# Attention over 39 fields: probabilities transposed as 32 fp32 products of 39x39 blocks in 64x64 tiles, in place of eight 103x103 transposes

## What is computed

```python
def _mhsa(x, Wq, Wk, Wv, Wr):          # x: [2048, 39, 64], HEADS = 2, dh = 32
    q = (x @ Wq).reshape(B, n, HEADS, dh)
    k = (x @ Wk).reshape(B, n, HEADS, dh)
    v = (x @ Wv).reshape(B, n, HEADS, dh)
    scores = jnp.einsum('bihd,bjhd->bhij', q, k)
    attn = jax.nn.softmax(scores, axis=-1)
    out = jnp.einsum('bhij,bjhd->bihd', attn, v).reshape(B, n, D)
    return jax.nn.relu(out + x @ Wr)
embed_x = emb_table[X + offsets[None, :]]
att = embed_x
for i in range(3):
    att = _mhsa(att, WQ[i], WK[i], WV[i], WR[i])
att_output = relu(att.reshape(B, FLAT) @ Wlin)
h = relu(embed_x.reshape(B, FLAT) @ W1 + b1)
h = relu(h @ W2 + b2)
dnn_output = relu(h @ W3 + b3)
return sigmoid(att_output + dnn_output)
```

## Time and profile before

| | |
|---|---|
| median of 3 runs | 2034.81 us |
| runs | 2032.1, 2036.02, 2034.81 us |
| span of the profiled execution | 2034.7 us |
| PE, multiplications busy | 94% |
| PE, weight loads busy | 83% |
| DVE busy | 83% |
| ACT busy | 66% |
| POOL busy | 44% |
| mean granted TensorE clock | 0.991 |

### The profile page before, as it was taken

How to read it: one execution, slowest core, us unless ns; L and a number is a source line. 1 busy time by engine, 2 the same in 40 slices (tenths; PEclk the granted TensorE clock), 3 DMA queues, 4 the chain that set the end, 5 groups by cost and what they waited for, 6 DMA issues and landing times.

```text
span 2034.7 us, 105018 instructions
## 1 busy us (share of the span) xinstructions
PE 1914.9 (94%) x44960; PEld 1692.9 (83%) x44960; DVE 1690.5 (83%) x3771; ACT 1351.5 (66%) x3609; POOL 893.3 (44%) x949
## 2 busy tenths in 40 slices
PE   1499999999999999999999999999999999999998
PEld 0387888888888888888888888888888888888887
DVE  3477889889898888979888898888889898888987
ACT  1366666667666676766766776666776667676665
POOL 6544354444535454354544435354453545444000
PEclk9899999999999999999999999999999999999998
DMA  4210111111111111111111111111111111110000
GB/s 113 60 31 25 31 27 32 29 30 31 28 33 28 31 30 29 32 28 32 29 30 30 29 33 27 32 28 30 31 28 34 28 32 29 30 31 26 20 20 16
DMA packets 67859, 64.71 MB, mean 32 GB/s; under 512 B 24056, under 2 KB 54792, under 8 KB 67400
## 3 DMA queue, kind: packets, MB, share of 16 engines
q1 hardware_dynamic: 47432, 37.52, 6.3%
q0 software_dynamic: 19968, 20.49, 5.3%
HBM read 27.24 MB, written 0.01 MB: 13 GB/s over the span
## 4 chain that ended last, share of the span: by engine, by line
PE 86%; DVE 5%; issue 4%; ACT 3%; another core or an unknown queue 1%; POOL 1%; SPq 0%; DMA 0%; ACTq 0%
PE SV L479 20%; PE Ob L496 14%; PE X L464 12%; PE X L457 8%; PE X L459 5%; PE X L458 5%; PE Mb L432 3%; PE Mb L433 3%; PE Mb L434 3%; PE Ob L457 3%; PE Ob L458 2%; PE Ob L459 2%; PE Ob L423 2%; PE Mb L450 1%
## 5 line engine op out<-in xcount | busy, mean ns | idle before, releaser
L355 POOL DMA_INDIRECT emb<-L_rec_emb_table,idx_t x624 | 646.9, 1037 | 752.4 <-PE Ob L496 551.2
L742 DVE TENSOR_REDUCE den<-sd 103x16 f32<-103x624 f32 x384 | 308.0, 802 | 225.6 <-ACT sd L616 211.0
L479 PE MATMUL SV<-yv,xs 64*39 64x142 f32 x12288 | 456.0, 285 | 21.2 <-ACT v_sb L618 13.4
L479 PEld LDWEIGHTS SV<-yv,xs 64*39 64x39 f32 x12288 | 349.8, 113 | 68.0 <-issue 39.6
L600 ACT ACTIVATE xs<-Ob 128x312 f32<-128x312 f32 x256 | 110.4, 431 | 383.6 <-PE Ob L496 383.6
L722 DVE TENSOR_REDUCE mx<-SV 103x8 f32<-103x312 f32 x768 | 332.7, 473 | 37.0 <-PE SV L479 28.7
L496 PEld LDWEIGHTS Ob<-pt,v_sb 39*32 39x32 f32 x12288 | 272.1, 106 | 96.5 <-issue 96.0
L464 PE MATMUL X<-ident,pn 103*103 103x103 f32 x3072 | 343.0, 255 | 0.0
L496 PE MATMUL Ob<-pt,v_sb 39*32 39x39 f32 x12288 | 326.4, 198 | 8.9 <-issue 8.5
L332 POOL COPY xs<-embT 64x256 f32<-64x256 f32 x300 | 239.1, 797 | 211.6 <-ACT embT L560 80.7
L727 DVE TENSOR_TENSOR sd<-SV,mx 103x312 f32<-103x312 f32 x768 | 330.2, 470 | 0.1
(11 more groups left out here) (81 smaller groups left out, 2749.2 us busy)
## 6 DMA issues: line engine op xcount, KB each, us to landing
v_x<-v_sb SPq DMA_DIRECT2D x768, 39.0 KB
emb<-L_rec_emb_table,idx_t POOLq DMA_INDIRECT x624
xs<-L_rec_W SPq DMA_DIRECT2D x19, 256.0 KB
w<-L_rec_W SPq DMA_DIRECT2D x1, 512.0 KB
idx_in<-r_X SPq DMA_DIRECT2D x1, 312.0 KB, 3.8
b_b<-L_rec_b SPq DMA_DIRECT2D x1, 256.0 KB
b_b<-L_rec_b SPq DMA_DIRECT2D x1, 128.0 KB
w_b<-L_rec_W SPq DMA_DIRECT2D x1, 128.0 KB
```

What stands on the lines that cost most here:

```text
L355: nc.gpsimd.indirect_dma_start(out=emb[:, n % ER, f % 2 * D:(f % 2 + 1) * D], out_offset=None, in_=table, in_offset=bass.IndirectOffsetOnA ...
L479: last = nc.tensor.matmul(SV[64 * b:64 * b + F, at:at + YR], x_pair(u, e, p), yv[64 * e:64 * e + D, l, p, :], start=True, stop=True, skip_ ...
L742: nc.vector.tensor_reduce(den[:], pe_sb[:], AX.X, ALU.add).then_inc(den_ready, 1)
```

## The change

The padding columns of `pn` go, and with them the memset of `pn` on POOL. `transposes(u)` does for each of the eight groups four products, one for each pair of sample b and head h: the block of 39x39 at partitions 64b is the stationary operand, an identity of 39x39 at the same partitions the moving one, and the output goes to partitions 64h of bank XB[b]. All are raised by one `t_ps`, not one for each half, and all wait for both copies of `yv`. XB[b], and so `pt`, is now split by the sample of a pair and not by group; ACT copies 312 columns that lie side by side. The attended products take the even pairs first, for which the first copy is enough, and then the odd ones.

```diff
--- before.py
+++ after.py
@@ -151,8 +151,8 @@
         pe_sb = sd
         den = sb("den", [KR, G, H])
         rd = sb("rd", [KR, G, H])
-        pn = sb("pn", [KR, PS, G, H, 64])
-        pt = sb("pt", [KR, G, 2, F])
+        pn = sb("pn", [KR, PS, G, H, F])
+        pt = sb("pt", [KR, 2, G, F])
         red = sb("red", [128, TILES * NP])
         w_in = red[0:D, 0:2 * L * D].rearrange("q (k d) -> q k d", d=D)
         wT = red[0:D, 2 * L * D:4 * L * D].rearrange("q (k d) -> q k d", d=D)
@@ -339,7 +339,6 @@
             pool.wait_ge(pre_pool, 3)
             nc.gpsimd.affine_select(out=ident[:], in_=ident[:], compare_op=ALU.not_equal, fill=1.0, base=0,
                                     pattern=[[-1, 128]], channel_multiplier=1).then_inc(pre_pool, 1)
-            nc.gpsimd.memset(pn[:], 0.0).then_inc(pre_pool, 1)
 
             def gather(t, f):
 
@@ -385,7 +384,7 @@
 
         @block.tensor
         def _(pe):
-            pe.wait_ge(pre_pool, 5)
+            pe.wait_ge(pre_pool, 4)
             pe.wait_ge(ld_w, LD_W)
             for k in range(2 * L):
                 nc.tensor.transpose(X0[0:D, k * D:(k + 1) * D], w_in[:, k, :], ident[0:D, 0:D])
@@ -458,12 +457,13 @@
                 nc.tensor.matmul(out_ps, w_lo[:, l, at:at + 128], x_hi[:, slot, :], start=False, stop=False)
                 return nc.tensor.matmul(out_ps, w_hi[:, l, at:at + 128], x_hi[:, slot, :], start=False, stop=True)
 
-            def transposes(u, j):
-
-                for g in range(G // 2):
-                    last = nc.tensor.transpose(XB[j][0:KR, g * 128:g * 128 + KR],
-                                               pn[:, u % PS, j * (G // 2) + g, :, :].rearrange("q h f -> q (h f)")[:, 0:KR],
-                                               ident[0:KR, 0:KR])
+            def transposes(u):
+
+                for g in range(G):
+                    for b, h in ((0, 0), (1, 1), (0, 1), (1, 0)):
+                        lo, po = 64 * b, 64 * h
+                        last = nc.tensor.matmul(XB[b][po:po + F, g * F:(g + 1) * F], pn[lo:lo + F, u % PS, g, h, :],
+                                                ident[lo:lo + F, lo:lo + F], start=True, stop=True, skip_group_check=True)
                 last.then_inc(t_ps, 1)
 
             def scores(u):
@@ -484,16 +484,17 @@
             def attended(u):
 
                 pe.wait_ge(v_moved[u % VS], 32 * (u // VS + 1))
-                for p in range(UP):
+                pe.wait_ge(pt_ready, 2 * u + 1)
+                for p in itertools.chain(range(0, UP, 2), range(1, UP, 2)):
                     j, pp, b = p // 4, p % 4 // 2, p % 2
-                    if p % 4 == 0:
-                        pe.wait_ge(pt_ready, 2 * u + j + 1)
+                    if p == 1:
+                        pe.wait_ge(pt_ready, 2 * u + 2)
                     for e in range(2):
                         g = (2 * j + e) * 2 + pp
                         for h in range(H):
                             lo, po = 64 * h, 64 * e + DH * h
                             v = v_sb[lo:lo + F, u % VS, h, g, :] if b == h else v_x[lo:lo + F, u % VS, g, :]
-                            last = nc.tensor.matmul(Ob[po:po + DH, p * F:(p + 1) * F], v, pt[lo:lo + F, g, b, :],
+                            last = nc.tensor.matmul(Ob[po:po + DH, p * F:(p + 1) * F], v, pt[lo:lo + F, b, g, :],
                                                     start=False, stop=True, skip_group_check=True)
                 last.then_inc(o_ps, 1)
 
@@ -525,9 +526,8 @@
                     embedding(*chunk_at(s), u < 0)
                 if 0 <= u < TOTAL:
                     pe.wait_ge(pn_ready, u + 1)
-                    for j in range(2):
-                        pe.wait_ge(y_ready, min(2 * s + j + 1, 2 * TOTAL))
-                        transposes(u, j)
+                    pe.wait_ge(y_ready, min(2 * s + 2, 2 * TOTAL))
+                    transposes(u)
                 if s < TOTAL:
                     pe.wait_ge(y_ready, 2 * s + 2)
                     scores(s)
@@ -622,10 +622,10 @@
                 u = s - PV_AT
                 if 0 <= u < TOTAL:
                     at_least(act, o_ps, u)
-                    for j in range(2):
-                        act.wait_ge(t_ps, 2 * u + j + 1)
-                        nc.scalar.copy(pt[:, j * (G // 2):(j + 1) * (G // 2), :, :].rearrange("q g b f -> q (g b) f"),
-                                       XB[j][0:KR, :].rearrange("q (n f) -> q n f", f=64)[:, :, 0:F]).then_inc(pt_ready, 1)
+                    act.wait_ge(t_ps, u + 1)
+                    for b in range(2):
+                        nc.scalar.copy(pt[:, b, :, :].rearrange("q g f -> q (g f)"),
+                                       XB[b][0:KR, 0:C]).then_inc(pt_ready, 1)
                 if converted_at(s):
                     convert_high(*converted_at(s))
             act.wait_ge(fin_pe, 2)
@@ -743,8 +743,8 @@
                 dve.wait_ge(den_ready, s + 1)
                 nc.vector.reciprocal(rd[:], den[:]).then_inc(rd_ready, 1)
                 dve.wait_ge(rd_ready, s + 1)
-                at_least(dve, t_ps, 2 * (s - PS + 1))
-                nc.vector.tensor_tensor(pn[:, s % PS, :, :, 0:F], pe_sb[:], rd[:, :, :, None].to_broadcast([KR, G, H, F]),
+                at_least(dve, t_ps, s - PS + 1)
+                nc.vector.tensor_tensor(pn[:, s % PS], pe_sb[:], rd[:, :, :, None].to_broadcast([KR, G, H, F]),
                                         ALU.mult).then_inc(pn_ready, 1)
                 if ts == H1T_AT - 2:
                     dve.wait_ge(l1_ps, t + 1)
```

## The result

| | before | after |
|---|---|---|
| median | 2035.41 us (4 runs, 2032.1 to 2038.5) | 2402.32 us (4 runs, 2398.59 to 2407.8) |
| span of the profiled execution | 2034.7 us | 2399.7 us |
| mean granted TensorE clock | 0.991 | 0.976 |

The change makes the kernel 18% slower: ratio 1.179, with a 95% interval of 1.177 to 1.182. The prediction was 2019 us, with a range of 2005 to 2041. It had the sign wrong, and its range missed the time by 361 us. The mechanism that it called rival 2 (PE starved for instructions) is the one that happened, but at 340 us where it was priced at 21; the forecast's own sum had no term for it.

The account below looks back on a forecast made before the run. It took PE and ACT's parallel way, nearly equal, to bound each stage; some 0.10 us saved on PE a stage gave 1.0 us a tile, 16 us over sixteen tiles: 2034.8 - 16 = 2019 us, range 2005 to 2041.

Parts of the forecast that it names:

- rival 2: New short PE records bring as many instruction-starved pauses as L496's, another 21 us: 2040 us; chance 0.12.
- The bound: From attended values to scores, PE's products and transposes run beside ACT's work, taking nearly the same time.
- ACT's parallel way: ACT's relu, casts, copies and exp up to the v_sb copy; decides the scores' start in nine of 24 stages.
- The pace of the products: New group: sixteen rounds of four records, 0.038 us each, 0.61 us; with the switch 0.71, against 0.82 for the transposes.
- The switch of 0.093 us: PE's price for going from full-width work to 64x64 tiles; moves from behind the group to ahead of it.
- Rival 3: Weight loads of the new products unhidden, 0.073 us a round, 154 us more: 2189 us; chance 0.07.
- What of it reaches the end: Nothing in nine stages of a tile, 0.41 us over six, 0.10 each in most of nine; 1.0 us a tile.
- nine starts of scores: Stages of one tile, mostly third layer, whose scores start over 0.1 us beyond the 0.145 us minimum behind v_sb.
- The start at 1084.40: Scores' start taken off the nine: exp there waits for VectorE's differences, so DVE takes what PE gives.
- the 16 us: Whole forecast gain: 1.0 us a tile over sixteen tiles, 2034.8 to 2019 us.
- The small edits: Single wait and pt copies, attended order, pn without padding or memset: cost or gain nothing.
- the cover: ACT's c_hi cast, needed stages later, and 1.44 us idle behind the pt copies; without it at most 0.3 us a stage.

Follow-up runs that it names:

- run 5: Changed kernel with pn and identity in bf16 (64 instructions fewer a stage) and no gathers for tiles 2 to 16: 2085.49 us, ratio 1.027.
- run 2: Kernel before without the gathers of tiles 2 to 16: 1987.04 us, ratio 0.979.
- run 3: Kernel before with the changed kernel's waits (transposes wait for both yv copies, ACT waits once for all eight): 2038.02 us, ratio 1.0035.
- run 1: Changed kernel without the gathers of tiles 2 to 16: 2315.97 us, ratio to before 1.141.
- run 4: Changed kernel with pn and identity in bf16, 64 instructions fewer a stage, gathers kept: 2138.38 us, ratio 1.055.
- run 10: Changed kernel with 78 moving columns in each of the 32 products and no gathers for tiles 2 to 16: 2328.26 us, ratio 1.147.
- run 6: Changed kernel with its gathers let go by the second pt copy, not by the end of the attended values: 2948.11 us, ratio 1.451.
- run 8: Kernel before with its gathers let go by the second pt copy, some 0.6 us earlier: 2805.83 us, ratio 1.379.

## Why the prediction was wrong

**The bound.** PE's chain and ACT's parallel way were read rightly from the earlier trace rows: run 5 shows both, scores behind v_sb in 96% of the stages once PE's way is shorter. What the reading left out is a third line beside the two, PE's own instruction stream. Nothing in the earlier trace rows shows it, because it was not late then.

**The pace of the products.** Right. 0.038 us a round and a hidden load: the clean group is 0.614 us, predicted 0.61; up to the scores 0.65 to 0.66, predicted 0.62 (and 0.61 and 0.093 make 0.70, not the 0.71 of the sum). The switch of 0.093 us moved ahead of the group as predicted (0.20 less 0.11 us). The sum took the scores to start as the sixteenth round ends, at 0.61 us; they start 0.038 us behind the last record instead, which itself starts at 0.614. So the saving is 0.07 us a stage and not 0.10. Rival 3, loads unhidden, did not happen. The rule of the Trainium skill, "TensorE: Matmul & The Clock Gate" (What overlaps and what doesn't), that a load overlaps running products only where the row group differs, would have the round of L465 at 0.07 us or more (an estimate from the prediction's 0.035 us for a load and 0.033 for the columns); the trace has 0.038.

**What of it reaches the end.** This step can't be judged by the changed kernel, in which few stages are free of pauses. Run 5 speaks for its kind of reading: nothing where ACT decides, a gain where the scores start later than that. Of the nine starts of scores that the prediction named for over 0.1 us of room, seven (places 19, 20, 22, 23, 0, 1 and 2) end a stage that is 0.15 to 0.35 us shorter in run 5 than in run 2. The eighth, at place 3, does not, and the ninth, at place 5, is the one with a pause in that tile alone. The start at 1084.40, which was taken off the nine for VectorE's sake, was never among them: its copy (start 1083.69, 0.56 us long) ends 0.145 us ahead of it, so ACT decides there. With 0.07 us a stage in place of 0.10 the 16 us were too many; how many would have come is not shown.

**The small edits.** "Cost nothing" holds within the resolution for all but the single wait: run 3 puts it at 0.35% (0.12 to 0.57%). The prediction allowed 0.3 us a stage if the cover were gone. ACT's waits there went from 11.2 to 103.4 us, and the kernel only by 7 to 9, so most of it lies in idle time, as the prediction said. The padding and the order of the attended products had no run of their own; between runs 1 and 2 the block ends leave 13 of 329 us for them and all else.

**Rival 2.** This is the term that failed. The sum of the forecast left the pauses out, and the rival took the 21.3 us in 51 pauses of the earlier trace rows as what 24,576 short records cost, and as many new ones as another 21 us. The measured price is 340 us, sixteen times that. Three things were wrong in it.

- A pause was priced by the record, as if each short record had a chance of its own to be late. What counts is how soon PE comes to the end of a block. A stage had some 244 instructions in PE's queue and now has some 356. The three groups of short records are 320 of them (128 in the products, 64 in the scores, 128 in the attended values, each multiplication with its load), and a stage without a pause runs through them in 2.4 us. The next block can't be had that fast: in every kernel its first instruction starts 2.14 us or more behind the start of its fetch, and the fetch starts, in the changed kernel, some 1.2 us (median) behind PE's reaching the end of the block before. Before, the eight transposes carried 16 instructions over 0.8 us, and the densest 256 instructions in a row took 4.3 us; now they take 2.0. The change took away precisely that rest. The earlier trace rows gave the warning: 359 blocks came one in 5.7 us then, and the shape of the burst was known. What they could not give is how soon a block can come.
- The cause of the pauses in the earlier trace rows was not looked for. 34 of the 57 belong to gathers and 5 to block ends. Had I set POOL's timeline beside one cluster, the question would have been what the gathers run beside. They run beside the transposes: eight records do not notice them (one pause in 81 gathers), 64 do (173 in 173). That moves 208 us of pauses into the new products.
- "The pauses come in clusters, and most stages have none at all" was held against the rival. It was the sign that a coincidence decides, and a change that fills the place of the coincidence will meet it in every stage.

The Trainium skill, "Runtime: NRT & Kernel Launch" (Instruction fetch mechanics), says that PE's instructions come in blocks of 16 KiB, 256 instructions, fetched ahead, so that crossing a block's end is mostly hidden. The size agrees with the traces (16.4 KB, pauses 256 apart). The hiding holds for the kernel before, 2.9 us in all, and fails for the changed one, 154 us, and 319 us in run 1. I leant on that sentence against the rival and did not ask how dense a burst it covers.

**How the chances were given.** Rival 2's time of 2040 came from its price, and with it the upper end of the range. A rival that says "a supply runs dry" has no upper bound in the few pauses of a kernel in which it has not run dry; its range should have been worked out from how soon the supply can come, or left open upwards.

## What to carry to other kernels

Count a change that splits matrix products also in instructions: every fp32 product of a small tile is two multiplications and two loads in PE's stream, and where PE runs through them faster than the next block comes (here 256 in 2.0 us, against 2.14 us and more from the start of a fetch, which itself starts late) it waits, whatever its busy share says. Look at the densest stretch, not at the mean, and leave long instructions between dense groups, so that the stream can catch up. When a trace shows pauses with no releaser, set the other engines' timelines beside one of them before pricing it: here a gather on POOL was running beside most of them, and moving a single gather of a tile gained 0.8%.

## What the runs showed of the hardware that was not expected

**PE's instructions come about one block ahead.** In each of the 13 kernels the instruction queue makes as many fetches as PE's stream has ends of 256 (527 and 527 in the changed kernel, 359 and 359 before), so fetches and block ends can be paired in order. A fetch takes 0.88 to 1.6 us (median 1.0). Take the time from the start of the fetch that belongs to one block end to PE's reaching the next end inside a group of short records. In all kernels together, 1048 ends were reached within 2.0 us: PE paused at every one. Of 3221 that were reached after more than 2.6 us it paused at 20. Of the 653 between, it paused at 225. Nine in ten of these pauses end 2.2 to 2.8 us behind the start of that fetch. In the stage at 1028.96 the fetch ran from 1029.71 to 1030.73, and PE went on at 1032.09, 2.38 us behind its start. That only one block is held ahead is inferred from these times; no run changed the block or the place of a program in it.

So a dense burst is not needed for such a pause if the fetch starts late. Behind PE's reaching a block's end it starts after 0.65 to 3.1 us (nine in ten in the changed kernel, median 1.2), later where that end lies in the attended values (median 1.7 us) than in the new products (1.0). Of the changed kernel's pauses at block ends over half (98 of 183, counted by the strict remainder) follow a block that lasted 3.5 us or more, and of run 5's 123 of 149. The rule of 3.3 to 3.5 us a block, by which the expectations of runs 4 and 10 went, is therefore too simple. It was read from the shortest distance of two fetches, 3.24 to 3.40 us in the kernels with the 32 products; in those with transposes it is 3.43 to 4.16, as they never ask sooner. What makes a fetch start late is open.

**A gather on GpSimd keeps PE from its instructions.** In the changed kernel a gather's first pause begins some 0.6 us behind its start, a pause is typically 0.65 us long, and the last one ends 0.3 to 0.6 us behind the gather's end. Between two such pauses mostly 8 to 11 instructions pass, as in the rows at 1010.53 and 1011.62. Wide work does not show it (none of 298 gathers that ran beside wide products alone has a pause); the 64 short records do at every gather (173 of 173 beside them alone). POOL's copies have no such effect. Moving the gathers by part of a stage cost 38% in the kernel before and 23% in the changed one (2948 against 2402 us). By what path a gather does this stays open: the traces show the coincidence and runs 1, 2, 6 and 8 that it goes and moves with the gathers, not the resource. A gather is work on POOL and traffic on the DMA engines (20.5 MB in all of them), and the runs remove or move both together.

**Work that costs nothing.** Doubling the columns of 12,288 products, 0.45 us in a group without a pause, left the time at 2395 us against 2402.

**The clock.** The changed kernel was granted 0.976 on average, and 0.97 from 1000 to 1100 us, where before had 1.00 (us, then busy us of PE, PEld, DVE, ACT, POOL with counts, clock, DMA share, GB/s; before, then after):

```profile
1000.00:1100.00 100.00, 98.61 (x2356) 87.39 (x2352) 87.36 (x197) 69.80 (x187) 43.54 (x48) 1.00 0.13 31
```

```profile
1000.00:1100.00 100.00, 90.02 (x2893) 75.91 (x2886) 71.92 (x157) 59.63 (x157) 42.42 (x46) 0.97 0.10 26
```

PE was idle for 10.0 us of this stretch and for 1.4 before. The mean of 0.97 is two short stretches at the lower of the two levels (1.2 GHz) and full speed (2.4 GHz) between them. The first comes right behind the paused group at 1009: PE had been busy for 1.90 of the 3.80 us from 1009.0 to 1012.8, at a clock of 1.00, and then ran at 0.50:

```profile
1012.90:1016.20 3.30, 3.30 (x94) 2.80 (x87) 2.17 (x6) 1.33 (x5) 0.44 (x1) 0.50 0.03 7
```

The scores take 14 us more than their pauses explain. At the lower clock the steps between their records are 0.054 us in place of 0.030, 255 steps in all, which makes 6 of the 14; the rest is open.
